# A transformer layer on one core: in each unit of the score maxima the mask products open the accumulation instead of closing it

## What is computed

```python
h = x @ W1 + b1                                  # q, k, v of 16 heads of d = 8
w = jnp.einsum('bhqd,bhkd->bhqk', q, k) / dk
mask = jnp.tril(jnp.ones((S, S), dtype=x.dtype))
w = jax.nn.softmax(w * mask - (1.0 - mask) * NEG_BIG, axis=-1)
a = jnp.einsum('bhqk,bhkd->bhqd', w, v)
...
x = x + attn(xn, ...) + ffn(xn, ...)
```

## Time and profile before

| | |
|---|---|
| median of 3 runs | 545.26 us (543.38 to 548.12) |
| the profiled execution, its own time | 544.02 us |
| its span, first to last instruction | 541.9 us |
| TensorE busy (matmuls) | 501.4 us, 93% |
| VectorE busy | 391.7 us, 72% |
| ScalarE busy | 336.2 us, 62% |
| granted TensorE clock, mean | 0.965 of full |
| reductions of the maxima (L1583), first to last | 18.0 to 292.8 us |

### The profile page before, as it was taken

How to read it: one execution, slowest core, us unless ns; L and a number is a source line. 1 busy time by engine, 2 the same in 40 slices (tenths; PEclk the granted TensorE clock), 3 DMA queues, 4 the chain that set the end, 5 groups by cost and what they waited for, 6 DMA issues and landing times.

```text
span 541.9 us, 13812 instructions
## 1 busy us (share of the span) xinstructions
PE 501.4 (93%) x4544; PEld 332.6 (61%) x4545; DVE 391.7 (72%) x787; ACT 336.2 (62%) x743; POOL 331.6 (61%) x392
## 2 busy tenths in 40 slices
PE   8879999999998999999989889999998899999994
PEld 3335554455454454544544389989998898877772
DVE  7796678997979978879885155556555556358886
ACT  2015788787767877777867665655555556365551
POOL 6369553442558878778788616667665574575442
PEclk9885799999979999999999999999999999999998
DMA  5434434240111544713111222222222222245555
GB/s 165 152 102 138 135 140 160 76 160 22 60 61 50 173 141 175 196 67 128 52 41 36 65 67 57 73 59 73 63 65 61 58 78 73 92 117 147 161 148 145
DMA packets 53978, 54.66 MB, mean 101 GB/s; under 512 B 6000, under 2 KB 40656, under 8 KB 53680
## 3 DMA queue, kind: packets, MB, share of 16 engines
q1 hardware_dynamic: 49248, 44.55, 26.6%
q0 software_dynamic: 4544, 9.35, 5.4%
q10 hardware_dynamic: 144, 0.20, 0.1%
HBM read 20.77 MB, written 18.68 MB: 73 GB/s over the span
## 4 chain that ended last, share of the span: by engine, by line
PE 60%; DVE 18%; issue 6%; DMA 4%; ACT 4%; another core or an unknown queue 3%; POOL 2%; ACTq 1%; DVEq 1%; SPq 0%
PE st_banks L875 12%; PE av_bank L902 11%; DVE neg_max L1583 11%; PE av_bank L1092 9%; PE mx_pair L1080 3%; PE mx_pair L1078 3%; PE mx_pair L1079 3%; DVE o_sb L1761 3%; PE mx_pair L859 2%; PE st_banks L784 2%; DMA out<-o_sb 2%; PE st_banks L790 2%; PE mx_pair L849 2%; PE st_banks L1080 1%
## 5 line engine op out<-in xcount | busy, mean ns | idle before, releaser
L1583 DVE TENSOR_REDUCE neg_max<-mx_pair 128x2 f32<-128x256 f32 (+3 forms) x256 | 200.4, 818 | 30.5 <-PE mx_pair L859 26.5
L1267 ACT ACTIVATE probs<-st_banks 128x512 f32<-128x512 f32 (+1 forms) x384 | 177.1, 528 | 59.7 <-PE st_banks L875 56.8
L875 PE MATMUL st_banks<-q_st,k_st 32*128 32x384 f32 (+3 forms) x512 | 118.3, 408 | 3.8 <-ACT probs L1267 2.5
L730 POOL DMA_INDIRECT y_tok<-y_sb,y_rows x78 | 78.1, 1001 | 68.9 <-ACT y_sb L1378 50.0
L875 PEld LDWEIGHTS st_banks<-q_st,k_st 32*128 32x128 f32 x512 | 59.5, 191 | 78.9 <-ACT probs L1267 50.1
L849 PE MATMUL mx_pair<-k_st,q_st 31*128 31x256 f32 (+3 forms) x512 | 92.0, 398 | 6.9 <-DVE neg_max L1583 5.1
L902 PE MATMUL av_bank<-probs,v_wide 128*18 128x128 f32 (+2 forms) x1272 | 97.4, 397 | 0.5 <-POOL probs L613 0.5
L654 POOL DMA_INDIRECT sorted_x<-xn_rows,slot_idx x64 | 63.6, 993 | 13.5 <-issue 12.9
L1092 PE MATMUL av_bank<-edn,hidT 128*128 (+1 forms) x468 | 59.9, 277 | 4.7 <-ACT y_sb L1378 3.5
L613 POOL TENSOR_SCALAR_AFFINE_SELECT probs<-probs 128x1024 f32<-128x1024 f32 x32 | 34.8, 1087 | 43.0 <-ACT probs L1267 42.9
L1092 PEld LDWEIGHTS av_bank<-edn,hidT 128*128 128x128 f32 (+1 forms) x468 | 55.2, 191 | 7.9 <-issue 7.9
(11 more groups left out here) (205 smaller groups left out, 900.9 us busy)
## 6 DMA issues: line engine op xcount, KB each, us to landing
sorted_x<-zeros SPq DMA_DIRECT2D x13, 387.0 KB, 3.3
xg<-sorted_x SPq DMA_DIRECT2D x39, 129.0 KB
picked<-y_tok SPq DMA_DIRECT2D x16, 256.0 KB, 3.9
q_st<-q_hi SPq DMA_DIRECT2D x14, 256.0 KB
k_st<-k_hi SPq DMA_DIRECT2D x14, 256.0 KB
egu<-in_e_gu SPq DMA_DIRECT2D x2, 1408.0 KB, 6.4
x_all<-in_x SPq DMA_DIRECT2D x8, 256.0 KB, 3.9
att_T<-a_T SPq DMA_DIRECT2D x8, 256.0 KB
```

What stands on the lines that cost most here:

```text
L730: pool.indirect_dma_start(y_tok, bass.IndirectOffsetOnAxis(ap=y_rows[:, t, k:k + 1], axis=0), y_sb[t % 2][:, k, :], None).then_inc(y_st[t ...
L875: ins = pe.matmul(st_banks[:, i % 3, lo:lo + w], k_st[buf][32 * j:32 * j + 32, g, kb * P:(kb + 1) * P], q_st[buf][32 * j:32 * j + 32, g, k ...
L1267: act.activation(dst, src, ACT.Exp, scale=SCALE).then_inc(st_free, 1)
L1583: ins = dve.tensor_reduce(neg_max[:, g, h:h + 2, qb], mx_pair[i % 2][:, :, lo:lo + (qb + 1) * P], AX.X, ALU.max, negate=True)
```

## The change

In each unit the mask products now come first, with `start=True`, after the wait for `mx_free`. The products of queries and keys follow directly, all with `start=False`, and the last of them raises `mx_full`. The hand-written order calls `max_masks` ahead of `max_scores`, both between the two heads' scores. Nothing else moves: no instruction is added or removed, and the other engines' streams stay as they were.

```diff
-                if i >= 2:
-                    pe.wait_ge(mx_free, i - 1)
-                for c, (qb, lo) in enumerate(MX_PARTS[u // 2]):
+                for qb, lo in MX_PARTS[u // 2]:
...
-                        pe.matmul(mx_pair[i % 2][:, k, lo:lo + w], q_st[buf][32 * j:32 * j + 31, g, qb * P:(qb + 1) * P],
-                                  k_st[buf][32 * j:32 * j + 31, g, 0:w], start=(c == 0), stop=False, skip_group_check=True)
+                        ins = pe.matmul(mx_pair[i % 2][:, k, lo:lo + w], q_st[buf][32 * j:32 * j + 31, g, qb * P:(qb + 1) * P],
+                                        k_st[buf][32 * j:32 * j + 31, g, 0:w], start=False, stop=True, skip_group_check=True)
+                ins.then_inc(mx_full, 1)
 
             def max_masks(n, u):
                 i = MX_NO["M", n, u]
                 lo, blocks = MX_DIAG[u // 2]
+                if i >= 2:
+                    pe.wait_ge(mx_free, i - 1)
...
-                    ins = pe.matmul(dst, mask_q[rows], mask_k[rows, 0:blocks], start=False, stop=True, skip_group_check=True)
-                ins.then_inc(mx_full, 1)
+                    pe.matmul(dst, mask_q[rows], mask_k[rows, 0:blocks], start=True, stop=False, skip_group_check=True)
...
                 if maxima:
+                    max_masks(s + 2, 0)
                     max_scores(s + 2, 0)
                 if scored:
                     scores(s, (3,))
-                if maxima:
-                    max_masks(s + 2, 0)
```

More of the change, by code:

```diff
@@ L958, in _ @@
                 if maxima:
+                    max_masks(s + 2, 1)
                     max_scores(s + 2, 1)
@@ L961, in _ @@
                     scores(s, (1,))
-                if maxima:
-                    max_masks(s + 2, 1)
                 if s < 0:
@@ L975, in _ @@
                 if maxima:
+                    max_masks(s + 2, 2)
                     max_scores(s + 2, 2)
@@ L978, in _ @@
                     scores(s, (7,))
-                if maxima:
-                    max_masks(s + 2, 2)
                 if s < 0:
@@ L987, in _ @@
                 if maxima:
+                    max_masks(s + 2, 3)
                     max_scores(s + 2, 3)
@@ L990, in _ @@
                     scores(s, (5,))
-                if maxima:
-                    max_masks(s + 2, 3)
                 if s == -2:
@@ L1011, in _ @@
                 if maxima:
+                    max_masks(s + 2, 4)
                     max_scores(s + 2, 4)
@@ L1014, in _ @@
                     scores(s, (11,))
-                if maxima:
-                    max_masks(s + 2, 4)
                 if valued:
@@ L1021, in _ @@
                 if maxima:
+                    max_masks(s + 2, 5)
                     max_scores(s + 2, 5)
@@ L1024, in _ @@
                     scores(s, (9,))
-                if maxima:
-                    max_masks(s + 2, 5)
                 if s == -2:
```

## The result

The changed kernel took 547.36 us (median of 20 executions, 542.91 to 551.11), the kernel before beside it 546.28 us (20 executions, 540.86 to 554.30). The ratio is 1.0061, with a 95% interval of 1.0034 to 1.0089. This ratio leaves disturbed executions out, and more of these fell on the kernel before: the means over all 20 of each are 547.19 us for the changed kernel and 547.09 for the one before. The forecast was 543.2 us, 0.4% faster; the time lies in the range and within 1% of before, but this comparison puts it on the other side: a change of the wrong sign, with 1.0 outside the interval. The experiments had to say whether that is the change.

A forecast was written before the change was run, and what follows sets the result against it. TensorE was taken to bound the attention most of the time, VectorE in pieces. TensorE -1.0, VectorE -1.0 and the `mx_free` wait 0 gave -2.0 us: 542.0 on the profiled execution, 543.2 for a median; range 537.5 to 549.0.

The forecast's parts named there:

- Theory B: From the experiments: masks first bring more time at half clock; expected 1.005 to 1.009 for the changed kernel again.
- How the numbers follow: Chances for the total: forecast 543.2 us 0.57; faster by over 1% 0.16, slower 0.08, within 1% 0.76.
- Term (a): How long units hold TensorE's array: units 0 and 1 +1.3 us, units 5 -1.5, units 4 -0.8; sum -1.0.
- The 28 units 5 are all like rows 6: Count in TensorE's sum: all 28 units 5 resemble one timeline excerpt and gain 0.055 us each, -1.5 us.
- Term (b): VectorE's maxima start earlier as masks no longer stand behind second scores: 0.4 to 2 us gain, taken as -1.0.
- Held back in line: Second scores start late behind products ahead of them in the program; if everywhere, +16, 560 us; chance 0.05.
- a third product: In units 4 and 5, only a strip's third product holds second scores back: 546 us for a median; chance 0.23.
- VectorE is the bound: VectorE paces the chain's TensorE pieces, so its shorter waits count fully: middle value 6 us, 538 us; chance 0.10.
- The clock: A half-clock piece at 150 to 160 us could vanish or come twice: 3.4 us either way; one less, chance 0.05.
- The rule on weight loads: Loads overlap running matmuls only when going to another row group; Term (a) would be 0, the total 543.0 us.

The follow-up runs named there:

- masks between: Kernel before with the masks directly behind the unit's own products, both ahead of the second scores, in all six units: 545.72 us, ratio 1.0007.
- masks between and first: Kernel before with masks behind the own products but ahead of the second scores in units 0 to 3, masks first in 4 and 5: 546.06 us, ratio 1.0012.
- the changed kernel with dummies: Changed kernel plus 24 more dummy products on TensorE at the start: 546.80 us, ratio 0.9938 to before.
- dummies at the start: Kernel before plus 24 more dummy products on TensorE, in rounds -2 to 0: 547.38 us, ratio 1.0027.

## Why the prediction was right or wrong, point by point

**Is the changed kernel slower?** Not by any comparison but the first, and the record speaks against it. It stood at 1.0061, 1.0034 and 0.9960 in three comparisons, before against itself at 1.003 and 0.9991. Theory B is refuted by the clocks: three traces of before have mean clocks of 0.965, 0.942 and 0.953, three of the changed kernel 0.950, 0.953 and 0.954, and over all executions whose clock was noted the mean is 0.9505 for before (123 executions) and 0.9514 for the changed kernel (44). In those of before the time is shorter by 4.2 us where the granted clock is higher by 0.01 (a straight line through them, correlation -0.91); at equal clock the changed kernel is 0.3 us shorter, with a standard error of 0.3. Twice the missing share of the clock, times the span, is the time at half clock: about 38, 64 and 51 us before, 55, 52 and 50 us after. The first pair of traces compared one of the warmest executions of before (three of the 123 have 0.965 or more) with an ordinary one of the change.

**The step that failed.** A gain of 2.0 us was forecast and the first comparison showed a loss, 1.1 us between the medians and 0.6% by the ratio. The failed step is the one in "How the numbers follow" that left the half-clock time out of the sum, gave a changed number of its pieces a chance of 0.05 and an effect of 3.4 us, and took the one profiled execution of before, plus 1.2 us for its median, as the base. The pieces change in every execution: the clock of before ranges from 0.930 to 0.969, and single times of before range over 13 us (540.86 to 554.30) beside the first comparison alone. A forecast of -2 us could hardly have been seen beside that, and the median of three that it started from lay 1.0 us below the one of 20. Why the first 20 against 20 came out 0.6% apart, with 1.0 outside the interval, is not shown further than that: the means over all of them are 0.1 us apart, and the comparison didn't come out so again. That the time fell into the range is no merit of the units' prices.

**Term (a), the hold of the array, -1.0 us.** The prices were right where they came from a start in the rows: +0.05 for units 0 and 1 (0.045 forecast), 0 for units 2 and 3, -0.05 for units 4. Units 5 ahead of the next scores take the forecast 0.40 to 0.41 where their second scores start with the rest. In about two of three these come 0.06 to 0.07 late and the unit takes 0.43 to 0.44. What the sum missed is ScalarE: units 4 and 5 got shorter, so the second scores of unit 5 arrive before the exponent that frees their bank has ended (211.20 in the rows above), and wait for it. "The 28 units 5 are all like rows 6" was also misread: in the trace of before 10 of them are followed by other work, and three at 267 to 282 us have late second scores.

**Term (b), VectorE's earlier start, -1.0 us.** The mechanism is there: the gap of the earlier trace rows is gone, and masks moved ahead of the second scores without changing the order in the strip gained 0.25 us over the twelve intervals that repeat, 1.2 over all 17. The size of VectorE's waits was misjudged. In 60 to 292 us they didn't fall from 20.5 us to 12 to 17:

```profile
DVE neg_max L1577 <- PE mx_pair L847: 21.9, 45, 1.2
PEld mx_pair L910 <- DVE neg_max L1577: 6.9, 16, 0.7
```

But this stretch holds half-clock time in either trace, and not the same. Between 160 and 270 us both ran at full clock; first before, then the changed kernel:

```profile
DVE neg_max L1583 <- PE mx_pair L859: 8.1, 21, 0.6
DVE neg_max L1577 <- PE mx_pair L847: 7.1, 21, 0.6
```

There the waits fell by an eighth, where 17 to 41% had been forecast. That what VectorE no longer waits for in one unit it waits for in the next may be the reason; it isn't shown. TensorE's wait for VectorE at L910 did fall, over 60 to 292 us from 8.2 to 6.9.

**The sum, -2.0 us.** Over the 17 intervals at full clock the three traces of before give 138.36, 138.48 and 138.25, the three of the changed kernel 137.94, 137.88 and 137.91: -0.45 us, and no trace of the one reaches a trace of the other. Scaled to the 29 rounds that have all their parts this is -0.8 us, an estimate. Right in sign, 0.4 of the size, and 0.15% of the time. Over the twelve intervals that repeat the change is worth -0.36, masks between -0.25, so the order in the strip is left with about -0.1. Each of the terms (a) and (b), -1.0 over 28 rounds, would be -0.43 over twelve (an estimate): (b) came out at about 0.6 of its size and (a) at a quarter. Within (a), masks first in 4 and 5 gained 0.57 on top of masks between, where 2.3 over 28 rounds is 1.0 over twelve. One piece went against the sum: interval 15 took 9.25, 9.24 and 9.27 us in the changed kernel and 8.70, 8.67 and 8.73 before. It took 9.23 in the kernel with masks between and first, and 8.63 in the changed kernel with dummies. So it isn't fixed by the order of the attention. In the five traces with 9.2 or more the projection (L784) in it starts 2.37 to 2.40 us after the transpose, in the others with masks after 1.95 to 2.09, and GpSimd's zeroing starts, behind a send of rows to the experts (L654), after 1.11 in place of 0.59. But masks first in 4 and 5 alone have GpSimd just as late and take 8.73, so that isn't it alone, and the cause stays open. Without this interval the gain would be 1.0 us over 16, twice as large.

**Rivals.** Held back in line: no, in either form. Second scores of unit 5 start 0.02 or 0.06 to 0.07 behind the first, under the 0.1 that I had named (a few near 266 to 275 us come later). The late ones stand 0.05 behind the end of an exponent each time; with masks between, three products deep in each strip too, they start at 0.02, and without masks, two deep, some come 0.08 late. They wait for ScalarE, not for a third product. VectorE is the bound: no; rounds shrank by 0.03 us each. The clock: that pieces come and go was right, but far too rare and too small as I put it, and nothing shows that the new order moves them.

**The rule on weight loads** in the Trainium skill (TensorE: Matmul & The Clock Gate, "Part 3: Packing small matmuls") would have made term (a) zero. The traces disagree: the loads of the own products at 213.12 run in the strips where the masks still are, and units 0 and 1 change by +0.05 and units 4 and 5 by -0.05 us (0.46 to 0.41 ahead of scores that aren't late), as overlapping loads predict. The 543.0 that the prediction gives for this rule is for the profiled execution; beside its 543.2 for a median stands 544.2.

## What to carry to other kernels

Before forecasting a change of under 1%, run the kernel against itself: if single executions spread over 2%, price the change on pieces of the trace that repeat (here rounds at full clock), say beforehand that the total won't show it, and check each piece by itself: five of 17 rounds here moved by up to 0.6 us without any change of the order, enough to turn round which of two kernels looks best. Inside a strip of the array what goes first should be long enough to cover the next weight load; and a product that another engine waits for should not stand behind one that may have to wait itself: that gave 0.25 of the 0.36 us over the twelve rounds that repeat. And a strip that gets shorter can run into the wait of another engine, as units 5 did into ScalarE's.

## What the runs showed of the hardware

Products in different strips start out of program order (203.13 ahead of 203.34 in the earlier trace rows), but count as done in order: VectorE started 0.08 us after the late scores ended, 0.26 after the masks' own record did. The clock's pieces at half speed come at similar places (near 40 and 540 us in all traces, near 153 and from 270 to 310 us in most), but their length varies from execution to execution of one kernel: 38 to 64 us in three traces of before. Within one kernel the time follows the clock closely (4.2 us for 0.01, over 123 executions). But clock gained by dummy products isn't speed by itself: 0.973 with dummies at the start went with a span of 541.9 us, the same span as 0.965 without.
